# Tap matrices of the FIR stage stored channel by channel instead of tap column by tap column

## The reference, cut to what matters

```
q, k, v = silu(conv4(hs @ W))                      # per sequence, 1024 x 256
fir = lambda x, w: causal_depthwise_conv(x, w)     # y[t, ch] = sum_j w[ch, j] x[t - (taps-1) + j, ch]
local_short = fir(v, fir_short_w)                  # 5 taps per channel
local_long  = fir(v, fir_long_w)                   # 64 taps per channel
# both feed the statistics, the gate and the weighted mix of the layer's output
```

## Time and profile before

| | |
|---|---|
| median of 3 runs | 6020.67 us (6015.63 to 6024.58) |
| the profiled execution | 6031.09 us, span of its instructions 6029.3 us |
| mean granted TensorE clock over the span | 0.926 of full speed |
| `phase_b` on PE, from its first product to its last | 2710.67 us to 3042.53 us of the span |
| the convolution's products (line 1155) | 286.9 us of PE time |
| the products that make the matrices (line 1140) | 32.1 us of PE time |

### The profile page before, as it was taken

How to read it: one execution, slowest core, us unless ns; L and a number is a source line. 1 busy time by engine, 2 the same in 40 slices (tenths; PEclk the granted TensorE clock), 3 DMA queues, 4 the chain that set the end, 5 groups by cost and what they waited for, 6 DMA issues and landing times. The chain is left out here.

```text
span 6029.3 us, 119845 instructions
## 1 busy us (share of the span) xinstructions
PE 5421.1 (90%) x42776; PEld 4326.3 (72%) x42776; DVE 4262.5 (71%) x13841; ACT 2668.0 (44%) x6214; POOL 2549.7 (42%) x3716
## 2 busy tenths in 40 slices
PE   6999999999999999979966645999999999999987
PEld 5888888888888888859954433777777777777765
DVE  4777777777777777752127885888887888888861
ACT  2555555555555555531133321444444444444441
POOL 1222222222222222210057751666666666666660
PEclk9999999999999999989965555999999999999998
DMA  1011101101110110118855542222222222222211
GB/s 41 29 34 36 33 31 36 36 29 34 36 36 29 34 36 29 34 39 186 201 140 147 141 111 63 61 62 61 61 61 61 61 61 62 61 62 61 61 35 44
DMA packets 603925, 373.22 MB, mean 62 GB/s; under 512 B 336528, under 2 KB 589264, under 8 KB 603344
## 3 DMA queue, kind: packets, MB, share of 16 engines
q1 hardware_dynamic: 532880, 329.91, 19.9%
q10 hardware_dynamic: 65664, 16.78, 1.2%
q0 software_dynamic: 4800, 18.88, 1.0%
HBM read 212.59 MB, written 137.10 MB: 58 GB/s over the span
## 5 line engine op out<-in xcount | busy, mean ns | idle before, releaser
L526 POOL TENSOR_TENSOR a_shift<-a_mean_var,a_eps 128x2 f32<-128x2 f32 x256 | 71.3, 278 | 1833.5 <-DVE a_mean_var L736 1833.5
L2125 PE MATMUL c_bank<-c_xT,c_gate 128*128 128x512 f32 x1024 | 499.8, 611 | 1.9 <-ACT c_statsT L1878 1.9
L750 DVE SCALAR_TENSOR_TENSOR a_cv<-a_raw,a_taps,a_cv 128x256 f32<-128x256 f32 x1152 | 461.9, 479 | 19.5 <-ACT a_cv L628 10.0
L820 PE MATMUL a_bank<-a_w,a_hidden 128*128 128x256 f32 x2048 | 459.1, 382 | 0.9 <-ACT a_hidden L613 0.9
L918 PE MATMUL a_bank<-a_turned,a_w 128*128 128x256 f32 x2048 | 453.0, 379 | 1.1 <-ACT a_turned L574 1.1
L820 PEld LDWEIGHTS a_bank<-a_w,a_hidden 128*128 128x128 f32 x2048 | 383.8, 190 | 71.8 <-issue 20.6
L918 PEld LDWEIGHTS a_bank<-a_turned,a_w 128*128 128x128 f32 x2048 | 384.0, 190 | 51.2 <-ACT a_turned L574 1.6
L1775 POOL TENSOR_TENSOR c_expd<-c_e,c_logit 128x16 f32<-128x16 f32 x128 | 371.7, 2904 | 51.1 <-DVE c_logit L1961 38.7
L1761 POOL TENSOR_TENSOR c_stats<-c_l2sq,half 128x16 f32<-128x16 f32 x128 | 373.4, 2917 | 17.8 <-DVE c_l2sq L1950 17.8
L2129 PEld LDWEIGHTS c_bank<-c_statsT,c_gate_stats 128*128 128x128 f32 x2048 | 270.1, 192 | 123.8 <-issue 123.8
L1345 POOL TENSOR_TENSOR i_coef<-i_base,i_exponent 128x12 f32<-128x12 f32 x128 | 298.6, 2332 | 76.7 <-issue 53.5
(11 more groups left out here) (294 smaller groups left out, 14194.1 us busy)
## 6 DMA issues: line engine op xcount, KB each, us to landing
a_x<-in_x SPq DMA_DIRECT2D x64, 256.0 KB, 3.3
scratch_xb<-a_xb SPq DMA_DIRECT2D x64, 256.0 KB, 2.1
scratch_q<-a_qkv_rows SPq DMA_DIRECT2D x64, 256.0 KB, 2.2
scratch_k<-a_qkv_rows SPq DMA_DIRECT2D x64, 256.0 KB, 2.7
scratch_v<-a_qkv_rows SPq DMA_DIRECT2D x64, 256.0 KB, 3.0
b_window<-scratch_v SPq DMA_DIRECT2D x8, 2048.0 KB, 22.2
scratch_long<-b_out ACTq DMA_DIRECT2D x8, 2048.0 KB, 24.6
scratch_short<-b_out POOLq DMA_DIRECT2D x8, 2048.0 KB, 18.4
```

The lines of the kernel that those rows point to most:

```text
L750: ins = dve.scalar_tensor_tensor(cv[s][:, n, c], raw[s][:, n, c, j:j + TOK], taps[:, n, c, j:j + 1], cv[s][:, n, c], ALU.mult, ALU.add)
L820: ins = pe.matmul(dst[:, t * D:(t + 1) * D], src[s][:, c, tile_cols(t)], weight[:, c], start=(c == 0), stop=(c == chunks - 1))
L2125: pe.matmul(dst[:].rearrange("p (h t) -> p h t", h=H), gate1[:, c, cols], xT[sl][:, c:c + 1].broadcast_to([P, H, P]), start=(c == 0), stop ...
```

## The change: what it does

The buffers `matrix` change their order of axes. Before, a partition held (kind, column i, channel), so the 128 columns of one channel's stationary operand lay 64 floats (256 bytes) apart. After, it holds (channel, kind, column i), and they lie side by side in 512 bytes. The copies out of PSUM write this order: the same 512 values per copy, read from the bank with the column i as the innermost index (512 bytes apart) and written in runs of four floats, one run every 256 bytes. The moving operand `window[h][:, :, c]` stays as it is, 128 values that lie 256 bytes apart. No instruction is added, removed or moved, and no wait changes.

```diff
-        matrix = [sb(f"matrix{g}", [P, K2, HALF, CH]) for g in range(2)]
+        matrix = [sb(f"matrix{g}", [P, CH, K2, HALF]) for g in range(2)]
...
-                    ins = copy(matrix[g % 2][:, :, m * COLUMNS:(m + 1) * COLUMNS],
-                               src[:].rearrange("p (i k c) -> p k i c", k=K2, c=CH))
+                    ins = copy(matrix[g % 2][:, :, :, m * COLUMNS:(m + 1) * COLUMNS],
+                               src[:].rearrange("p (i k c) -> p c k i", k=K2, c=CH))
...
-                        taps_of = matrix[g % 2][:].rearrange("p k i c -> p (k i) c")[:, :, c]
+                        taps_of = matrix[g % 2][:, c].rearrange("p k i -> p (k i)")
                         ins = pe.matmul(dst[:, (c - q * QUAD) * N:(c - q * QUAD + 1) * N], taps_of, window[h][:, :, c],
                                         start=True, stop=True)
```

## The result

| | before | after |
|---|---|---|
| median | 6019.91 us (4 runs, 6015.63 to 6024.58) | 5985.3 us (4 runs, 5981.71 to 5985.45) |
| the profiled execution | 6031.09 us | 5985.45 us |

The ratio is 0.9936, with a 95% interval of 0.9924 to 0.9949: 34.6 us less, where 35 were forecast. (A fourth run of the kernel before has joined the three in the table ahead of the prediction; the profiled execution of the changed kernel is one of its four.) The total is right to a microsecond; two of its terms were each wrong by a third or more, and in opposite directions.

What follows compares the result with a forecast made beforehand. PE was taken to bound phase_b, its passes slowed by how their operands lie. Passes 45.1 us off, less 10 of window waits and 0 for copies, made 35 off: 6020.7 to 5986 us, range 5966 to 6012.

Steps and rivals of the forecast that it cites:

- PE sets the phase's length, and a faster pass is worth its full time until the window is late: phase_b: PE is busy all the time, so what it gains shortens the program; 45.1 us gain on PE.
- The load and the moving read disturb each other only in the same place: Convolution passes in phase_b: reads at the same place of their rows slow passes to 0.286 us, against 0.236 otherwise.
- 236 ns per pass: Convolution's 1024 passes: pace falls from 280 to 236 ns, 45.1 us off; bounds 132 and 280 ns.
- The copies cost nothing: The 64 copies from PSUM into the matrix buffers: cost zero, 691 ns on DVE, 598 on ACT; upper bound 13 us.
- The window is late by 10 us in all, at units 3, 5 and 7: phase_b window transfers: waits of 1 to 3 us at units 3 and 5, some 7 at 7; together 4 to 14.
- A: Rival on phase_b's passes: the moving operand alone holds the pace, time stays 6021 us; chance 0.12.
- D: Rival on copies into the matrix buffers: slower, at 1.6 times costing 13 us; with rival A 6034 us; chance 0.05.
- C: Rival on phase_b's passes: pace falls to 132 ns, transfers become the bound, 75 us off, 5946 us; chance 0.08.
- B: Rival on phase_b's passes: straight load still disturbs; half the disturbance left gives 258 ns, 22 us gain, 6001 us; chance 0.13.

Runs made afterwards that it cites:

- e3: Kernel before with the second matrix buffer starting 16 bytes and the second window buffer 32 bytes later in their rows; 5994.65 us.
- e4: Kernel before with the second matrix buffer starting 64 bytes and the second window buffer 128 bytes later in their rows; 5992.05 us.
- e11: Kernel before with only the start of both matrix buffers moved 32 bytes later in their rows; 5981.6 us, ratio 0.9932.
- e2: Changed kernel's buffers and copies, but products read 128 floats 256 bytes apart (not a channel's taps); 6028.0 us, beside 6023.1 for the kernel before.
- e6: Kernel before with each column of the matrix buffers padded from 64 to 68 floats, so the stationary operand lies 272 bytes apart; 5984.2 us.
- e7: Changed kernel with each window padded from 64 to 68 floats, so the moving operand lies 272 bytes apart; 5993.2 us, ratio 0.9954.

## Why the prediction was right, and where it wasn't

*PE sets the phase's length, and a faster pass is worth its full time until the window is late.* Right: 60.8 us less on PE (60.3 of passes, 0.5 of the making), less 20.4 of waits, is 40.4, and the phase is 40.1 shorter.

*The load and the moving read disturb each other only in the same place.* Right, and shown by moving the place in both directions (e3, e4, e11). That also answers the rule of the Trainium skill weighed in the prediction, that loading takes no read bandwidth from the running product ("TensorE: Matmul & The Clock Gate", "Part 2: What happens when you issue a matmul"): it held at places 16 bytes or more apart, 28.1 us per unit, and failed at equal ones, 36.0 us.

*236 ns per pass.* Mis-sized: 221. I took the eighth pass of a bank and the last pass of all as undisturbed. They weren't. The profile of before shows the last pass with its own load (ns min/median/max, first and last start):

```profile
L1155 PE MATMUL b_bank<-b_window,b_matrix x2: 410/442/473, 3041.8 to 3042.1; 128*128 128x128 f32 x2
L1155 PEld LDWEIGHTS b_bank<-b_window,b_matrix x1: 390/390/390, 3041.9 to 3041.9; 128*128 128x128 f32 x1
```

The load that started at 3041.9 ran 390 ns, into the pass that started at 3042.1. There are 1024 loads for 1024 passes, and this is the last of them; it was that pass's own, and slow. In the profile after, the last pass takes 393 ns:

```profile
L1155 PE MATMUL b_bank<-b_window,b_matrix x1: 393/393/393, 3003.6 to 3003.6; 128*128 128x128 f32 x1
```

The same shows in e3: the pass behind the one disturbed pass takes 0.41 us too. So 410 ns is, as I now read it, the length of a pass whose start is still disturbed; an undisturbed one takes 393 to 397. The term became 286.9 - 226.6 = 60.3 us instead of 45.1. The load came out at 206 ns where I had named 192.

*The copies cost nothing.* Right, 691 and 597 ns, and e2 shows it for itself.

*The window is late by 10 us in all, at units 3, 5 and 7.* Mis-sized and partly misplaced: 20 us, at units 4, 6 and 7, and the wait at unit 7 was the shortest of the three, not the longest. The reason for lateness, 4 us or more of overlap between one window's copy and the next unit's transfers, was right. I let the older transfer pay for it. SP's issues in the profile after show who paid:

```profile
2799.53 0.58 SPq L1036 DMA_DIRECT2D b_window<-scratch_v  x1
2822.20 0.60 SPq L1040 DMA_DIRECT2D b_window<-b_window  x1
2827.67 0.58 SPq L1036 DMA_DIRECT2D b_window<-scratch_v  x1
2857.88 0.60 SPq L1040 DMA_DIRECT2D b_window<-b_window  x1
```

Unit 3's window (load at 2799.53, copy at 2822.20) was ready by 2835.04 without a wait; its copy landed 12.6 us after the issue, though the load for unit 4 began beside it, and the copy for unit 2, with no load beside it, took 12.7. Unit 4's load, issued while that copy ran, took 30.2 us where its forerunner took 22.7, and with the copy behind it the window was there at 2870.7, 43 us after it was asked for. Between the units lay 35.7 us, so PE waited 7.4. The loads for units 5, 6 and 7, each begun beside a copy, took 29.1 to 30.3 us likewise, and that for unit 2, begun beside none, 22.4. The shorter unit (28.3 us instead of my 30.2) added its 2 us to each.

Sum of the terms: forecast -45.1 + 10 = -35; measured -60.8 + 20.4 = -40.4 in the phase, and 34.6 by the medians. The difference of 6 us is within what the unchanged later phases scatter. That the total agrees to a microsecond is luck on top of a right mechanism.

The rivals: A (the moving operand alone holds the pace) and D (slower copies) are refuted. C names the true bound behind this one: the transfers, though at 221 ns and not at 132. B's half disturbance was not there: of the 62.4 us between equal places (286.9) and parted ones (224.5), the straight load leaves 2.1.

## What to carry to other kernels

When two operands are read with one large distance, ask not only whether each is scattered but whether both stand on the same place of their rows at the same time; a few bytes of offset can be worth the whole rearrangement. Look for the one instruction in eight that is faster than its neighbours: it is an experiment that the kernel makes for you, but check what its own load was doing before you take its length as the undisturbed one. And when an engine gets faster, lay the transfers on the new, shorter grid and ask which of them pays for the overlap; here it was the newest.

## What the runs showed of the hardware

- A pass of 128 float32 columns that lie 256 bytes apart goes every 219 ns beside a scattered load (310 ns) and every 221 beside a straight one (206 ns for most); with both operands in the same 16-byte place it goes every 286, the mean of the seven such passes of a bank. Offsets of +16, 32, 64 or 128 bytes between the two are free; at -16 one pass in eight meets the place of the next load.
- The pace of the scattered passes is the same at either clock: 20 in 4 us at 0.50 and at 1.00 (e11).
- 272 instead of 256 bytes between the floats does not make a scattered read faster: 330 ns instead of 310 for the load (e6, e11), 230 instead of 221 for the pass (e7, after).
- Copies out of PSUM whose innermost step is 512 bytes took the same 691 ns (DVE) and 597 ns (ACT) as straight ones (after, before).
- With the stores of a unit under way, a 2 MB load begun beside a 1.9 MB copy inside SBUF took 29.1 to 30.3 us, one begun beside none 22.4 or 22.7; the copy took 12.6 and 12.7 (after).
- Rows in SBUF 272 instead of 256 bytes apart made the first window's load take 15.7 us (2712.01 to 2727.67) instead of 12.6 (2711.05 to 2723.69).
